# Ten one-batch embedding sums: x loaded eight tiles at a time, and its sign bits written back over it

## The reference

```
embs = [dot(x, w) for x, w in zip(xs, ws)]
emb_sum = embs[0] + ... + embs[9]
q_emb = sum of dot(x ** 2, w ** 2) over the tables
fm = 0.5 * (emb_sum ** 2 - q_emb)
out = concatenate([fm] + embs, axis=-1)        # 1024 by 704
```

## Time and profile before

| what | value |
|---|---|
| median of 3 runs | 278.0 us |
| span of the profiled execution, first to last instruction | 276.5 us |
| what lies around the span, against the median | 1.5 us |
| bytes moved by DMA | 113.93 MB, mean 412 GB/s |
| queue q1 (SP: x, stores) | 11952 packets, 106.96 MB, 92.5% of the 16 engines' span |
| queue q10 (ScalarE: weights) | 5424 packets, 6.79 MB, 6.8% |
| last bytes of x landed | about 267.5 us |

### The profile page before, as it was taken

How to read it: one execution, slowest core, us unless ns; L and a number is a source line. 1 busy time by engine, 2 the same in 40 slices (tenths; PEclk the granted TensorE clock), 3 DMA queues, 4 the chain that set the end, 5 groups by cost and what they waited for, 6 DMA issues and landing times.

```text
span 276.5 us, 2773 instructions
## 1 busy us (share of the span) xinstructions
PE 219.0 (79%) x894; PEld 154.3 (56%) x894; DVE 222.7 (81%) x144; ACT 226.3 (82%) x284; POOL 117.5 (42%) x83
## 2 busy tenths in 40 slices
PE   0449978699998867968886887887688788689995
PEld 0327746477776555646664654654555565566752
DVE  3677967887798888878978978977987987999873
ACT  0758799899998788989868868867877877899984
POOL 0446665866324109347324134134044041083925
PEclk9995899999999999999999999999999999999999
DMA  6999999999999999999999999999999999999996
GB/s 247 424 406 425 410 433 422 418 430 428 419 423 424 430 415 409 432 428 419 429 421 432 421 427 427 425 421 423 422 428 433 424 413 424 409 417 408 406 399 230
DMA packets 17391, 113.93 MB, mean 412 GB/s; under 512 B 3168, under 2 KB 4448, under 8 KB 11232
## 3 DMA queue, kind: packets, MB, share of 16 engines
q1 hardware_dynamic: 11952, 106.96, 92.5%
q10 hardware_dynamic: 5424, 6.79, 6.8%
HBM read 110.85 MB, written 2.88 MB: 411 GB/s over the span
## 4 chain that ended last, share of the span: by engine, by line
DMA 66%; issue 14%; ACT 11%; PE 5%; ACTq 1%; POOLq 1%; POOL 1%; DVE 0%; SPq 0%
DMA x_ring<-in_x_dram 57%; DMA whole<-in_w_dram 9%; ACT is_set L414 8%; PE sums L552 4%; ACT whole L406 1%; POOLq L209 1%; PE sums L569 1%; POOL is_one L532 1%; ACT turned L425 1%; ACTq L393 1%; ACT results L430 0%; ACTq L401 0%; DVE is_one L648 0%; ACTq L400 0%; ACT turned L474 0%
## 5 line engine op out<-in xcount | busy, mean ns | idle before, releaser
L648 DVE TENSOR_SCALAR_CACHE_REDUCE is_one<-x_ring 128x4096 uint8<-128x4096 f32 (+2 forms) x64 | 218.9, 3436 | 46.2 <-DMA x_ring<-in_x_dram 44.7
L414 ACT ACTIVATE is_set<-x_ring 128x2048 fp32r<-128x2048 uint32 (+2 forms) x112 | 191.1, 1709 | 31.4 <-DMA x_ring<-in_x_dram 31.3
L552 PE MATMUL sums<-is_set,low 128*128 128x512 f32 x396 | 135.1, 423 | 54.2 <-ACT is_set L414 48.5
L552 PE MATMUL sums<-is_set,high 128*128 128x512 f32 x396 | 127.6, 404 | 0.0
L552 PEld LDWEIGHTS sums<-is_set,low 128*128 128x128 f32 x396 | 69.6, 193 | 93.9 <-issue 41.7
L508 POOL CAST high<-whole 128x1024 fp32r<-128x1024 f32 (+5 forms) x31 | 27.1, 874 | 141.9 <-ACT whole L406 141.9
L552 PEld LDWEIGHTS sums<-is_set,high 128*128 128x128 f32 x396 | 76.6, 193 | 18.7
L510 POOL TENSOR_TENSOR low<-whole,high 128x1024 fp32r<-128x1024 f32 (+5 forms) x31 | 60.7, 1960 | 2.5
L414 ACT ACTIVATION_READ_ACCUMULATOR is_set<-x_ring 128x1 f32 x112 | 21.1, 188 | 0.0
L406 ACT ACTIVATE whole<-whole 128x512 f32<-128x512 f32 (+5 forms) x31 | 16.6, 535 | 5.2 <-DMA whole<-in_w_dram 5.2
L521 POOL TENSOR_TENSOR total<-total,turned 128x1024 f32<-128x1024 f32 x8 | 19.2, 2402 | 0.0
(11 more groups left out here) (38 smaller groups left out, 14.8 us busy)
## 6 DMA issues: line engine op xcount, KB each, us to landing
x_ring<-in_x_dram SPq DMA_DIRECT2D x39, 2048.0 KB, 20.8
x_ring<-in_x_dram SPq DMA_DIRECT2D x20, 512.0 KB, 17.9
x_ring<-in_x_dram SPq DMA_DIRECT2D x6, 1024.0 KB, 21.2
whole<-in_w_dram ACTq DMA_DIRECT2D x19, 256.0 KB, 9.9
x_ring<-in_x_dram SPq DMA_DIRECT2D x3, 1536.0 KB, 21.7
out_dram<-results SPq DMA_DIRECT2D x9, 256.0 KB, 9.1
x_ring<-in_x_dram SPq DMA_DIRECT2D x4, 256.0 KB, 14.0
whole<-in_w_dram ACTq DMA_DIRECT2D x2, 192.0 KB, 6.5
```

What stands on the lines that cost most here:

```text
L414: nc.scalar.activation(is_set[chunk.k % SETS][:, 0:length], in_ring(chunk.place, length).bitcast(U32), ACT.Sign, accum_out=set_counts[:, c ...
L552: last = nc.tensor.matmul(sums[:, summing(n, half), :], w, x[:, at:at + HALF], start=first, stop=False, skip_group_check=True)
L648: nc.vector.tensor_scalar(is_one[c % 2][:, 0:length], in_ring(at, length), 1.0, None, ALU.is_equal, ALU.add, accum_out=one_counts[:, c:c + ...
```

## The change

The loads of x are of eight tiles (rows of 32 KB) in the large tables, one load per group as a rule, in a ring of 32 tiles. Table 2, the last, begins with one such load; 4, 2, 2, 1, 1 and two tiles in halves follow. A chunk is of four tiles. is_set is the ring's own memory under another type: ScalarE writes its zeros and ones over x, so it waits until VectorE has counted that chunk (`ones_counted`, no longer `x_landed`), and SP waits until TensorE has multiplied a chunk before it loads over it. The last two groups ("late") are written elsewhere in the ring and wait for their landing alone. Tables are padded to whole tiles by the host, so a table's last tile needs no loads of its own. The number of tiles that are loaded stays 199. The weights' load is issued after a group's first chunk and squared after the second chunk of the next group. GpSimd's parts have three buffers, not four.

```diff
-FULL = [2, 2, 2, 2]
+FULL = [[4, 4]]
 ORDER = [
-    (8, [[1, 1]]),
+    (8, [[[2]]]),
...
-    (1, [FULL] * 6 + [[1]]),
-    (6, [[2, 2, 2, 1, 1]]),
-    (0, [FULL] * 12 + [[1, 1]]),
-    (2, [FULL, [2, 1, 1, 1, 1], [1, 1, 1, 1, H]]),
+    (1, [FULL] * 6 + [[[1]]]),
+    (6, [FULL]),
+    (0, [FULL] * 12 + [[[2]]]),
+    (2, [FULL, [[2, 2], [2], [2]], [[1], [1], H]]),
 ]
-LOAD = 4
-RING = 20
-SETS = 5
-PAIRS = 4
+RING = 32
+PAIRS = 3
...
+            at = 0 if at + n * BATCH > RING * BATCH else at
+            loads.append(Load(len(loads), group.table, tile, n, chunks, at))
...
+        load.free = max([other.chunks[-1].k + 1 for other in had] + [0])
...
+        with nc.sbuf_tensor("is_set", [P, RING * BATCH], F32R) as is_set:
+            pass
         x_ring = sb("x_ring", [P, RING * BATCH], F32)
-        is_set = [sb(f"is_set{i}", [P, CHUNK * BATCH], F32R) for i in range(SETS)]
...
-                    sp.wait_ge(ones_counted, free)
-                    sp.wait_ge(set_counted, COUNTS[free - 1].chunks[-1].k + 1)
+                    sp.wait_ge(x_multiplied, free)
...
             def count_set(chunk):
-                act.wait_ge(x_landed[chunk.load.land], 16 * (chunk.load.turn + 1))
-                if chunk.k >= SETS:
-                    act.wait_ge(x_multiplied, chunk.k - SETS + 1)
+                if chunk.late:
+                    act.wait_ge(x_landed[chunk.load.land], 16 * (chunk.load.turn + 1))
+                    act.wait_ge(x_multiplied, LATE_FREE)
+                else:
+                    act.wait_ge(ones_counted, chunk.k + 1)
...
-                    if c == min(1, len(group.chunks) - 1):
+                    if c == 0:
                         if group.g + AHEAD < NGROUPS:
                             load_w(GROUPS[group.g + AHEAD])
-                    if c == min(2, len(group.chunks) - 1) and group.g + AHEAD - 1 < NGROUPS:
+                    if c == min(1, len(group.chunks) - 1) and group.g + AHEAD - 1 < NGROUPS:
                         square(GROUPS[group.g + AHEAD - 1])
```

More of the change, by code:

```diff
@@ L83, in __init__ @@
         self.land, self.turn = i % LANDS, i // LANDS
[L86 to L93, removed]
 class Group:
-    def __init__(self, g, place, table, tile, sizes, k):
+    def __init__(self, g, place, table, tile, k, loads):
         self.g, self.place, self.table, self.tile = g, place, table, tile
@@ L115, in __init__ @@
-        self.before = P - TAIL[table] if tile + at == TILES[table] > 1 else 0
-        self.loads = 1 + (self.tiles > 1) + 1 if self.before else 1
+        self.parts, at = [], 0
+        for sizes in loads:
+            own = []
+            if sizes == H:
+                own = [Chunk(k + half, self, at, 1, half) for half in range(2)]
+                at += 2
+            else:
+                for n in sizes:
+                    own.append(Chunk(k + len(own), self, at, n))
+                    at += n
+            k += len(own)
+            self.parts.append(own)
@@ L120, in plan @@
+        self.chunks = [chunk for own in self.parts for chunk in own]
+        self.tiles, self.end = at, k
 def plan():
@@ L133, with plan_loads @@
 NGROUPS, NCHUNKS = len(GROUPS), len(CHUNKS)
-def plan_counts():
-    lists = []
+COUNTED = [chunk for chunk in CHUNKS if chunk.half is None]
+NCOUNTS = len(COUNTED)
+def plan_loads():
+    loads, at = [], 0
     for group in GROUPS:
[L140 to L176, removed]
-    for load in loads:
[L179 to L182, removed]
@@ L185 @@
-LOADS, COUNTS = plan_counts()
-FINAL = COUNTS.pop()
-NCOUNTS = len(COUNTS)
+        if group.table == LAST and group.tile == 0:
+            at = 0
+        for chunks in group.parts:
+            tile = group.tile + chunks[0].at
+            if chunks[0].half is not None:
+                for half, chunk in enumerate(chunks):
+                    chunk.place = at + half * HALF
+                    for i in range(2):
+                        loads.append(Load(len(loads), group.table, tile + i, 1, chunks,
+                                          chunk.place + i * BATCH, half * HALF, HALF))
+                    chunk.load = loads[-2]
+                at += 2 * BATCH
+                continue
+            n = sum(chunk.n for chunk in chunks)
+            at = 0 if at + n * BATCH > RING * BATCH else at
+            loads.append(Load(len(loads), group.table, tile, n, chunks, at))
+            for chunk in chunks:
+                chunk.load, chunk.place, at = loads[-1], at, at + chunk.length
@@ new lines, in plan_loads @@
+    for load in loads:
+        had = [other for other in loads[:load.i] if other.chunks is not load.chunks and
+               (other.land == load.land or
+                other.at < load.at + load.length and load.at < other.at + other.length)]
+        load.free = max([other.chunks[-1].k + 1 for other in had] + [0])
+    late_at = dest = at
+    for chunk in CHUNKS:
+        chunk.dest = chunk.place
+        if chunk.group.table == LAST and chunk.group.tile:
+            chunk.late, chunk.dest, dest = True, dest, dest + chunk.length
@@ L195 @@
-FLAG_MAX = P * sum(TILES) * BATCH
+FLAG_MAX = P * sum(N_TILES) * BATCH
 def due(k, after):
@@ L526, in _ @@
             for half in range(2):
-                for load in FINAL.loads[2 * half:2 * half + 2]:
+                for load in FINAL[2 * half:2 * half + 2]:
                     pool.wait_ge(x_landed[load.land], 16 * (load.turn + 1))
```

146 lines of the change are left out of this document (55 added, 91 removed).

## The result

The changed kernel takes 295.25 us (median; 294.11 to 297.6), the kernel before 278.11 us on the same chip: ratio 1.0627, 95% interval 1.0605 to 1.0648. The forecast was 293.0 with a range of 282 to 301.

The account below looks back on a forecast made before the run. The kernel was taken to be bound by a short start, x's bytes at DMA pace and a 9 us end. Span 276.5 - 3.9 (rows) + 4 + 5 (stalls) + 10 (end) = 291.6, plus 1.5: 293 us, range 282 to 301.

Parts of the forecast that it names:

- Rows, -3.9 us: Loads of x: fewer, longer rows, 312 fewer per engine, save 3.9 us (bounds 0 and 5.3).
- 12 ns a row: Fixed cost of each row on a DMA engine, worked out together with a rate of 27.3 GB/s.
- Weights, 14.9 us: Weight loads of 256 KB land in 14.9 us behind 32 KB rows of x, before 9.9 (bounds 9.9 and 17.7).
- First stall, 4 us near 56: Near 56 us, load 9 needs load 5 multiplied; DMA idle for about 4 us (bounds 0 and 9).
- Second stall, 5 us near 135: Near 135 us, ScalarE waits 8.8 us for table 0's first weights; DMA loses 5 us (0 to 8).
- L+8.0: 8.0 us after table 1's last eight tiles land (L): ScalarE's first count ends, table 0's first weights are issued.
- The end, +10: After the last x lands, ScalarE's chain ends last: 19.3 against 9.0 us, 10 more (bounds 7 and 12).
- Sum: Whole kernel: 276.5 - 3.9 + 4 + 5 + 10 = 291.6 us of span; with 1.5 to the median, 293 us.
- (a): Rival for x loads: queue cuts rows to 16 KB, weights land in 9.9 us, no stalls; 286 us, chance 0.25.
- (b): Rival in large groups: weights at 17.7 us or TensorE's lower clock, 9 us late, longer stalls; 303 us, chance 0.11.
- (c): Rival at load borders: 34 fewer save 10.2 us, no stalls; 274 us; chance 0.09 including all faster or level.

Follow-up runs that it names:

- e3_weights_early: Changed kernel with weights asked for one group sooner (fourth weights buffer, one of VectorE's two given up), rows still 32 KB: 291.12 us.
- e10_loads4_small: Changed kernel with four-tile loads, two-tile loads in table 0's last three large groups and the last table's first two, result copy one chunk later: 276.63 us.
- e2_rows16: Changed kernel with each eight-tile load issued as two of four (rows of 16 KB), both waited for and freed together: 290.51 us.
- e11_w_halves: Changed kernel with each load of weights issued as two of half the columns, same bytes in twice as many rows: 335.76 us.
- e4_take_later: Changed kernel with ScalarE's copy of a table's turned sums (L382) one chunk later, TAKE_AFTER 3 to 4: 291.68 us.
- e9: Changed kernel with each eight-tile load made two of four tiles, each with its own chunk, landing and release: 285.53 us.
- e1: Changed kernel with the last table's first sixteen tiles loaded and counted two at a time: 291.08 us.
- e5: Changed kernel with weights asked for one group sooner and the last table in two-tile loads, without the later result copy: 285.83 us.
- e6: Changed kernel with weights one group sooner, result copy one chunk later and the last table in two-tile loads: 288.84 us.
- e8: e6 with the last six large groups of table 0 also loaded two tiles at a time: 281.8 us.

## Why the prediction was right, point by point

- **Rows, -3.9 us.** The last x comes 3.1 us sooner where the DMA never runs dry (e3_weights_early), within the bounds. That it is the number of rows is not shown: e10_loads4_small gains 2.5 us with only 72 rows fewer per engine, weights included, which by the forecast's 12 ns a row is 0.9 us.
- **Weights, 14.9 us.** Measured 14.5. Eight rows of weights that each let a row of x by was the right picture; e2_rows16 and e11_w_halves show it from both sides. The Trainium skill, page "DMA: Bandwidth & Descriptors", section "Queues, rings and completion order", says that an engine goes round between its queues a packet at a time; the runs agree (e2_rows16 has 9.7 us at 16 KB, the changed kernel 14.5 at 32 KB). There a packet is typically 9 to 17 descriptors; in this trace a turn is one row (batches 1.29 us apart).
- **First stall, 4 us near 56.** Measured 4.2, where it was forecast. The size was right partly by luck: table 3's weights landed at 33.7 us by the trace, not at 36, and the sum left out that L382 waits 4.23 us at 40 us for TensorE, which is on its lower clock until 38.3 us. Without that wait (e4_take_later) most of the gap is gone.
- **Second stall, 5 us near 135.** In the right place, and mis-sized: 1.4 us. ScalarE waited 4.71 us for the weights, not 8.8. The step that failed: "ScalarE's first count there ends at L+8.0 ... and it issues the weights". The trace has the issue at 107.81, the start of that count, which ends at 111.4; the weights are under way 3.6 us sooner. The earlier trace rows don't show this, but the trace before has it: a count starts at 150.06 us and lasts 1.92, and the issue at 150.19 falls into it.
- **The end, +10.** Measured +11.7. The last x came at T+15.7 (15.6 forecast, T the landing of the last table's eight tiles at 256.4), the last half tile at T+26.9 (26.9), and L382 waited 2.52 us (2.3). The rest of the difference is in the estimate of before's last landing (about 267.5, measured 268.07; so ScalarE's last half tile was not 0.6 us behind it but level) and in 1.0 us more behind ScalarE's last half tile (9.0, forecast 8.0).
- **Sum.** Span 291.6 forecast, 292.3 measured, partly by luck: the second stall, 3.6 us too large in the sum, was made up by the end (1.7 more), the rows (0.8 less gained) and the slow rows of x at the gaps (1.7), which the sum did not have. From the span to the time are 3.1 us (295.43 of this execution), not the 1.5 taken over from before. Of the edits, e3, e4, e9 and e11 have about 3.1 as well and e1, e2, e5, e6, e8 and e10 about 1.7; why is open.
- **The rivals.** (a), rows cut to 16 KB, falls: the trace has 2688 packets of 32 KB on the queue of x, 128 for each of the 21 large loads, 1.22 us each. e2_rows16, which has what (a) supposed, has no stalls as (a) said, but it takes 290.5 us, not 286: its end is 22.3 us, where (a) had 19 as in the forecast, and some 2 us of that come with TensorE's lower clock. (b) falls as a whole: no steady loss in the large groups (share 1.00 in 150 to 230 us), though TensorE's clock does fall in the gaps, as it said. (c) falls: the rate in the steady part is 427 GB/s, 0.7% up, worth 2 us and not 10. The Trainium skill, same page, section "Measured (HBM→SBUF, 128 partitions, SWDGE, issued from GpSimd)", has larger transfers faster; with a full queue this case shows almost nothing of it.

## What to carry to other kernels

When one queue's rows are made longer, look for small rows of another queue on the same engines: each of them waits for a long one, and whoever waits for that small load must ask for it sooner. When an engine is made to follow another over the same data, the size of the step is paid at the end of the stream, and it must be made small well before the end, until the slower of the two has caught up. Before a stall is put down to one wait, take the others in the same queue into the sum.

## What the runs showed of the hardware that was not expected

- **A queue of small rows has a pace of its own.** With rows of 32 KB, a group's weights (eight rows per engine) need eight rows of x to pass, 8 x 1.29 = 10.3 us with their own, and a group of x has just eight. In e6_all the weights of successive groups arrive 10.4 us apart: what is once late stays late, until x itself runs dry near 100 us (314 GB/s in the two slices from 93 to 108 us) and three loads of weights land between 98.8 and 100.7 us.
- **A DMA issue goes out while ScalarE's preceding count still runs**: issue and count both start at 107.81 us, and the count lasts 3.62.
- **A dry DMA queue costs more than its dry time.** Rows of 32 KB that start at a gap take up to 2.3 us instead of 1.22. In the changed kernel slow rows add 1.7 us to the 5.6 of the two gaps. Why they are slow is open.
- **TensorE's granted clock.** In the changed kernel it falls to the lower of its two levels, 1.2 GHz, from 17.8 to 38.3 us, again from 123.6 to 130.4, where the engine had been idle for 5.63 us, and for 3.4 us in four other places; before the change only from 19.5 us for 10 us and at the very end. Pairs of matmuls there (start, us):

```profile
126.47 1.19 PE L502 MATMUL sums<-is,low 128*128 128x512 f32 x2 [5.63 <-POOL low L461]
...
128.31 1.05 PE L502 MATMUL sums<-is,low 128*128 128x512 f32 x2
129.16 1.05 PE L502 MATMUL sums<-is,high 128*128 128x512 f32 x2
...
130.68 0.62 PE L502 MATMUL sums<-is,high 128*128 128x512 f32 x2
```

The pairs start 0.85 us apart on the lower level and 0.47 on the higher one, so here a stall of weights is followed by a slower TensorE just when the ring waits for it. In e2_rows16 such a fall lies in the last table and costs some 2 us.
